# A third probability buffer and new ranks and spans in the order planner of a two-layer attention kernel

## What is computed

```python
# layer 0, per image: full attention over the 4096 positions, channels 64 for the scores
e1, e2, asm = prelu(w1 @ gn(x)), prelu(w2 @ gn(x)), prelu(wa @ gn(x))
x = x + softmax(e1.T @ e2) @ asm                      # 4096 x 4096 scores
# layer 1, per image: causal additive attention, 16 tanh units for each pair of positions
t = ln(tokens(x))
scores[i, j] = sum_a w2[a] * tanh(f[i, a] + g[j, a] + b1[a]) + b2      # only j < i is kept
t = t + (exp(scores) / sum) @ t
# gate (softmax over positions, top 8 for each of 64 experts), expert FFN, scatter back
```

## Time and profile before

| | us |
|---|---|
| median of three runs | 5871.09 (5862.58 to 5873.55) |
| the profiled execution | 5872.08 |
| its span, first to last instruction | 5869.9 |
| PE busy | 5078.5 (87%) |
| ACT busy | 4930.1 (84%) |
| DVE busy | 2663.9 (45%) |
| POOL busy | 2001.5 (34%) |

### The profile page before, as it was taken

The page is one execution under the profiler, slowest core; times in us unless marked ns, Lnnn a source line. Parts: engine busy times, 40 slices in busy tenths (PEclk is TensorE's granted clock), DMA queues, the critical chain, the costliest instruction groups (busy, mean ns, idle before and its releaser), DMA issues. The chain is left out here.

```text
span 5869.9 us, 71555 instructions
## 1 busy us (share of the span) xinstructions
PE 5078.5 (87%) x28567; PEld 1726.0 (29%) x28567; DVE 2663.9 (45%) x3558; ACT 4930.1 (84%) x4186; POOL 2001.5 (34%) x1643
## 2 busy tenths in 40 slices
PE   6999988889999978899999987889999987666657
PEld 2333332223333323222333333222333332111113
DVE  8853474433454466443453466443354454000132
ACT  0139969999989969999959969999978969999970
POOL 1474431125454431113464441112555451111110
PEclk8999999999999999999999999999999999888977
DMA  0000000000000010000000010000000010000028
GB/s 29 12 18 8 8 29 1 1 8 6 13 19 10 9 40 8 1 1 8 19 19 4 12 44 8 1 1 8 10 22 10 12 38 17 1 1 1 6 101 283
DMA packets 39418, 123.99 MB, mean 21 GB/s; under 512 B 4464, under 2 KB 5424, under 8 KB 31984
## 3 DMA queue, kind: packets, MB, share of 16 engines
q1 hardware_dynamic: 38272, 119.03, 6.1%
q10 hardware_dynamic: 816, 0.39, 0.0%
HBM read 89.85 MB, written 29.56 MB: 20 GB/s over the span
## 5 line engine op out<-in xcount | busy, mean ns | idle before, releaser
L890 ACT ACTIVATE tanh_slots<-query_part,key_part 128x2048 f32<-128x2048 f32 (+41 forms) x3072 | 4151.5, 1449 | 149.0 <-DVE key_part L1293 101.5
L946 PE MATMUL ps<-tanh_slots,packed 128*32 128x512 f32 (+2 forms) x18432 | 2080.7, 588 | 457.4 <-ACT tanh_slots L890 449.5
L846 POOL TENSOR_TENSOR context_and_exp_sums<-context_and_exp_sums,exp_scores 128x512 f32<-128x512 f32 (+3 forms) x544 | 632.8, 1185 | 2043.4 <-ACT exp_scores L902 1615.5
L946 PEld LDWEIGHTS ps<-tanh_slots,packed 128*32 128x32 f32 x18432 | 541.2, 113 | 1931.1 <-ACT tanh_slots L890 1094.3
L1369 DVE TENSOR_TENSOR _tokens_second_and_probs<-ps,e_and_minus_max 128x1024 f32<-128x1024 f32 x512 | 624.5, 1220 | 1059.5 <-PE ps L981 534.4
L859 POOL TENSOR_TENSOR conv_prob_sums<-conv_prob_sums,_tokens_second_and_probs 128x512 f32<-128x512 f32 x480 | 613.6, 1278 | 1151.6 <-ACT _tokens_second_and_probs L907 1146.5
L981 PE MATMUL ps<-_tokens_second_and_probs,asm_tokens 128*128 128x512 f32 x2048 | 995.6, 612 | 6.8 <-ACT _tokens_second_and_probs L907 6.8
L907 ACT ACTIVATE _tokens_second_and_probs<-_tokens_second_and_probs 128x1024 f32<-128x1024 f32 x512 | 549.2, 1073 | 454.2 <-DVE _tokens_second_and_probs L1369 454.1
L1345 DVE TENSOR_REDUCE row_max_parts<-ps 128x1 f32<-128x1024 f32 x512 | 608.4, 1220 | 452.6 <-PE ps L1060 440.6
L1205 DVE TENSOR_TENSOR context_and_exp_sums<-context_and_exp_sums,ps 128x512 f32<-128x512 f32 (+3 forms) x544 | 344.7, 638 | 717.6 <-PE ps L957 713.3
L861 POOL TENSOR_TENSOR conv_prob_sums<-conv_prob_sums,_tokens_second_and_probs 128x512 f32<-128x512 f32 x480 | 617.6, 1287 | 37.7
(11 more groups left out here) (156 smaller groups left out, 2062.4 us busy)
## 6 DMA issues: line engine op xcount, KB each, us to landing
y_scratch<-residual_chunks SPq DMA_DIRECT2D x64, 256.0 KB, 2.0
tanh_slots<-in_wg SPq DMA_DIRECT2D x16, 1024.0 KB, 10.5
residual_chunks<-y_scratch SPq DMA_DIRECT2D x63, 256.0 KB, 2.7
residual_chunks<-in_x SPq DMA_DIRECT2D x32, 256.0 KB, 2.8
e_and_minus_max<-p_scratch SPq DMA_DIRECT2D x32, 256.0 KB, 3.3
query_part<-in_x SPq DMA_DIRECT2D x4, 1024.0 KB, 6.0
normed_tokens_first<-in_x SPq DMA_DIRECT2D x4, 1024.0 KB, 8.5
p_scratch<-e_twice SPq DMA_DIRECT2D x4, 1024.0 KB, 6.8
```

The source lines that it names most:

```text
L846: pool.tensor_tensor(dst, dst, src, ALU.add).then_inc(s_ds, 1)
L890: nc.scalar.activation(S[:, 4 * (R % 2) + k, q:SUP], F[:, SUP * blk.s + q:SUP * blk.s + SUP], ACT.Tanh, bias=keypart(blk.b, kg, kg + 1)).t ...
L946: last = mm(PS[32 * k:32 * k + 32, t, off:CHUNK], w2k[:, g, :], S[:, 4 * (R % 2) + k, CHUNK * t + off:CHUNK * t + CHUNK], start=(g == 0), ...
```

## The change

A third probability buffer `XPB` is a tile of its own, and pair P uses buffer P mod 3; `SM` of pair P now waits for `PV` and `PS` of pair P-3. `QK` gets rank 2.5, so that on TensorE it goes ahead of `C`, `F2a`, the `L` steps and `M`, but not of TR. The spans given to the planner are new: tanh 0.19 us and not 0.1 beside the same slope, `E`, `K`, TR, `C`, `M`, `SM`, `EX` and `PS` by some hundredths, the HOP 0.12 and not 0.08. No instruction is added or removed.

```diff
+NPB = 3
-    HOP = 0.08
+    HOP = 0.12
-                prior_t = put("ACT", "T", (R, k), 0.1 + 0.833e-3 * (SUP - x.start(k, g)), behind, 4)
+                prior_t = put("ACT", "T", (R, k), 0.19 + 0.833e-3 * (SUP - x.start(k, g)), behind, 4)
-                prior_tr = put("PE", "TR", (R, t), 0.03 + 0.86 * w, behind, 2)
+                prior_tr = put("PE", "TR", (R, t), 0.02 + 0.89 * w, behind, 2)
-                put("PE", "QK", (P,), 1.1, behind, 4)
+                put("PE", "QK", (P,), 1.1, behind, 2.5)
-                if P >= 2:
-                    behind += [("PE", "PV", P - 2), ("POOL", "PS", P - 2)]
-                put("DVE", "SM", (P,), 1.25, behind, 1)
+                if P >= NPB:
+                    behind += [("PE", "PV", P - NPB), ("POOL", "PS", P - NPB)]
+                put("DVE", "SM", (P,), 1.2, behind, 1)
+        XPB = sb("probs_third", [128, 2, CHUNK])
+        PROBS = [PROB[:, 0, :, :], PROB[:, 1, :, :], XPB[:, :, :]]
-                z = PROB[:, P % 2, :, :]
+                z = PROBS[P % NPB]
-                if P >= 2:
-                    dve.wait_ge(s_pv, P - 1)
-                    dve.wait_ge(s_ps, P - 1)
+                if P >= NPB:
+                    dve.wait_ge(s_pv, P - NPB + 1)
+                    dve.wait_ge(s_ps, P - NPB + 1)
...
```

More of the change, by code:

```diff
@@ L252, in plan @@
             behind += [("PE", "C") + es[i - NEB], ("POOL", "D") + es[i - NEB]]
-        prior_e = put("ACT", "E", (n, t), 0.12 + 0.45 * w, behind, 1)
+        prior_e = put("ACT", "E", (n, t), 0.19 + 0.43 * w, behind, 1)
         done = [prior_e]
         if t == x.diag:
-            done.append(put("DVE", "K", (n, t), 0.35, [prior_e], 0))
-        put("PE", "C", (n, t), 0.05 + 0.86 * w, done, 3)
+            done.append(put("DVE", "K", (n, t), 0.3, [prior_e], 0))
+        put("PE", "C", (n, t), 0.07 + 0.88 * w, done, 3)
         behind = [("PE", "C", n, t)]
@@ L332, in conv @@
                     behind += [("PE", "M", b, 0), ("DVE", "M", b, NPAIR - 1 if b else 0)]
-                put("PE", "QK", (P,), 1.1, behind, 4)
+                put("PE", "QK", (P,), 1.1, behind, 2.5)
                 behind = [("PE", "QK", P), ("DVE", "SM", P - 1) if P else None, ("SP", "bc", b, c) if p == 0 else None]
-                if P >= 2:
-                    behind += [("PE", "PV", P - 2), ("POOL", "PS", P - 2)]
-                put("DVE", "SM", (P,), 1.25, behind, 1)
-                put("ACT", "EX", (P,), 1.0, [("DVE", "SM", P), ("ACT", "EX", P - 1) if P else None], 2)
+                if P >= NPB:
+                    behind += [("PE", "PV", P - NPB), ("POOL", "PS", P - NPB)]
+                put("DVE", "SM", (P,), 1.2, behind, 1)
+                put("ACT", "EX", (P,), 1.05, [("DVE", "SM", P), ("ACT", "EX", P - 1) if P else None], 2)
                 behind = [("ACT", "EX", P)]
@@ L343, in conv @@
                     behind.append(("PE", "F2a", (cc - 2) // NCH, (cc - 2) % NCH))
-                put("POOL", "PS", (P,), 2.6 if p else 1.3, behind, 3)
+                put("POOL", "PS", (P,), 2.7 if p else 1.3, behind, 3)
                 behind = [("ACT", "EX", P)]
@@ L404, in prep @@
             behind = [("DVE", "Ev", b, NCH - 1)] + max_free(b) if m == 0 else [("PE", "M", b, m - 1)]
-            put("PE", "M", (b, m), 0.9, behind + [("DVE", "M", b, m - 2) if m >= 2 else None], 4)
-            put("DVE", "M", (b, m), 1.25, [("PE", "M", b, m), ("DVE", "M", b, m - 1) if m else None], 4)
+            put("PE", "M", (b, m), 1.0, behind + [("DVE", "M", b, m - 2) if m >= 2 else None], 4)
+            put("DVE", "M", (b, m), 1.18, [("PE", "M", b, m), ("DVE", "M", b, m - 1) if m else None], 4)
         for i in range(parts(b)):
@@ L851, in PS_ @@
                 pool.wait_ge(s_pe, P + 1)
+                src = PROBS[P % NPB]
                 if p == 0:
@@ L980, in PV @@
                 for u in range(2):
-                    last = mm(PVB, VT[:, 2 * p + u, :], PROB[:, P % 2, u, :], start=(p == 0 and u == 0),
+                    last = mm(PVB, VT[:, 2 * p + u, :], PROBS[P % NPB][:, u, :], start=(p == 0 and u == 0),
                               stop=(p == PPC - 1 and u == 1))
```

8 lines of the change are left out of this document (4 added, 4 removed).

## The result

The changed kernel takes 5657.9 us (median of 4 runs, 5654.5 to 5662.1) against 5870.9 before: a ratio of 0.964, 95% interval 0.9623 to 0.9657. That is 213 us less; 124 were forecast, and the range ended at 5695. The direction held, the size did not.

The account below looks back on a forecast made before the run. TensorE's work ahead of each gate was the bound where ScalarE starves, ScalarE where TensorE idles. 24 x 2 + 16 + 64 - 4 = 124 us off 5872.1 gave 5748 us; range 5695 to 5835, leaving out a tenth each side.

Parts of the forecast that it names:

- What bounds the kernel: TensorE's work ahead of each gate where ScalarE starves, ScalarE where TensorE idles; moving pairs beside tanh gains.
- The cause, the tanh span,: Planner's full-tile tanh span, 1.81 us against 1.90 measured, put TR too early; TensorE stands 0.41 us before each group.
- The row-maximum stage: Beside second-half tanh: 12 `M` per key block for 11, hidden in idle; 32 us less, which pairs then fill.
- The gap and the stretch of pairs: Images 2 and 3: 13 more pairs ahead cut the 86.5 us gap to 47; 24 us gained each at 4% idle.
- The first one: Image 1's gap closes, with ten more pairs ahead of it: 16 us, bounds 5 and 21.
- The first halves: Four times: two pairs fewer 4 us, idle to 4% 7 us, chain 5 us; 16 us each, 64 together.
- The chain behind the last chunk: End of each first half: ten TR and two `C` inside gain 5 us; 22 us latency stays, nothing shortens it.
- The head: Before the first tanh: pays 4 us for two `QK` and one `PV` more before the first `L5`.
- The tail: The last 1,000 us, without pairs: 0 change, between -3 and +3 us.
- The mask: GpSimd mask operations: denser pairs make more masks wait, some 10 us of VectorE beside TensorE's path, left out of the sum.
- all goes as the counts say: Rival: idle near 1 or 2%, 5690 us, below 5700; chance 0.12.
- Exponentials: Rival: `EX` placed too early on ScalarE stalls tanh, then TR and `L5`; 5896 us at 0.4 us each; chance 0.06.

Follow-up runs that it names:

- the fastest kernel: Kernel before with tanh constant 0.215, third buffer and QK at rank 2.5, other spans and HOP of before: 5598.0 us (0.9537).

## Why the prediction was wrong

**What bounds the kernel** held. TensorE made up pairs in the gaps while it stood idle beside tanh, and the gain came from there: in the stretch of image 1's second half and image 2's first half its idle went from 98.3 + 31.8 us to 68.1 + 11.2. ScalarE's idle up to the last half image was to fall by about 120 us and fell by 206.

**The cause, the tanh span,** was named ("the old was 1.81", "TensorE stands before TR"), but only as the reason for the row-maximum stage and as a doubt about a rival. The sum took the counts of the whole order, and the text left the credit with "the third buffer and the later TR". Experiments gave the tanh constant by itself 213 us, as much as the whole change, and the buffer by itself 7, hardly clear of noise.

**The row-maximum stage** held: 12 `M` in a key block of 32.6 us, hidden. TensorE is idle 24.2 us of the 340.0, for 23 taken.

**The gap and the stretch of pairs** held in mechanism. The gap is 46.8 us (47 forecast). The idle that I took as 4% was 2.3%, 8.8 us for 15, which is most of why a second half and gap won 34.0 and 27.5 us and not 24. The first one won 16.6 for 16.

**The first halves are the step that failed**: "Idle of TensorE in the 367 us goes from 5.9% to the same 4%: 7 us", 16 us each with the rest, measured 37.3, 34.0, 30.1 and 30.4. I took one idle share for both kinds of half, carried over from the gap's row, and treated the tanh error as 5%. But the error is 0.09 us for each tile, whatever its length. A first half has 256 tiles of 1.18 us mean, an error of 23 us in some 300; a second half 512 tiles of 1.58, 46 in 810:

```profile
L890 ACT ACTIVATE tanh_slots<-query_part,key_part 128x2048 f32<-128x2048 f32 (+51 forms) x256 | 275.5, 1179 | 5.1 <-DVE key_part L1293 2.7 <-PE ps L946 2.4
```

(ScalarE's groups of the kernel before, 3089.5 to 3432.8 us.) The busy time of this row counts the end of a tile that the next instruction overlaps. Taken from the start of each tile to the start of what follows, waits left out, the 256 tiles are 267.8 us in the trace; the planner had 244.8 with 0.1 and has 267.9 with 0.19. For the 512 of a second half it is 753.1, 707.2 and 753.2. So 0.19 is right for short tiles and long ones. That this error costs first halves time of their own was shown by changing it there alone: 389.2 became 369.6 us, 20 for the 23 that the planner had wrong. Buffer and rank with the old spans took 7 us off the same half (382.3). The two together are near the 30 of the change, though no run shows that they add up. In image 1 pairs in hand may take part, as they do in the run with 0.19 in second halves alone. The whole idle of a first half, chain included, fell from 31.8 to 11.2 us, 3.1%; my own lower bound (none) had given 30 us. Its 9.5 us less work (357.4 to 347.9 busy) was more than the 4 of the two pairs' counts; an `FAa` and a `C` now stand behind `L5`, and the granted clock, 0.69 over the chain in the earlier trace rows, is 1.00 over the whole half now. How the 9.5 us divide among these was not measured.

**The chain behind the last chunk** was to stay late ("22 us of latency ... which nothing here shortens"). Tanh was laid beside all but 3 us of it. I counted ten TR as 5 us of TensorE's work, and should have counted them as ScalarE's tiles, which is what waited.

**The head** was -6.8 for -4, but not for the reason given. The kernel with buffer and rank and old spans has the same two `QK` and one `PV` more in that chain, and its first tanh starts at 434.0 us, against 432.2 before; with tanh 0.19, buffer and rank it is 432.8. It is 439.7 where the small spans and HOP are in as well without the tanh span, and 439.6 with the small spans but the old HOP; yet small spans, HOP and tanh span without buffer and rank give 433.8. So the small spans cost the head some 6 us, and only together with buffer and rank; HOP costs it nothing.

**The tail** won 8.0 us where I said 0, -3 to +3: from the start of the last half image to its last tanh it is 845 us and not 853. Not investigated.

**The mask**: 227/293/1373 ns least, median and longest, for 278/293/1368, and 75.1 us in all for 72.6. So the masks are 2.5 us longer in sum, and the median not at all. The Trainium skill's page SBUF — State Buffer (SBUF: two separate sides) has a VectorE operation with two SBUF inputs and a GpSimd operation that reads SBUF exclude each other. By that rule I had allowed some 10 us more of masks; the trace shows 2.5, and not what caused them.

**The rivals**: "all goes as the counts say" (5690, below 5700) had 0.12 and came nearest; with no idle at all the sum had been 5657. That this meets the measured 5657.9 is luck: idle is left everywhere, the first halves won more than that bound gave them (131.7 for 120), the later second halves less (61.6 for 78), and the tail 8 for 0. Exponentials did not stall tanh: ScalarE waited 21.0 us for scores from the first tanh of image 2 to its second half before, and 1.7 + 1.1 us now; the longest such waits lie in the head. The range reached down to 5695 although the bound of no idle, worked out at 5657, is what the text asked it to take in.

## What to carry to other kernels

Where an order is laid out by a planner, compare its span for the commonest stage with the trace first, as an error for each instruction and not as a share: 0.09 us on 3,072 tiles was 276 us of planner's error and 213 us of time. Then sweep that one number past the measured value too: it is also a knob for how far other work is packed ahead of that stage. Of the five values tried here the best was 0.215 for a measured 0.19; that it is best where neither of the two busiest engines runs dry first fits the traces but is not shown. Test the parts of a change one by one even when the whole gains: here two of them gained 25 us and two lost 26, unseen in the sum. A buffer more gains nothing clear of noise while the order doesn't use it. When a text has both ends of an unknown share, the range has to reach them.

## What the runs showed of the hardware

TensorE was kept busy through mixed work better than I took from the trace before: in the stretch of 509 us (2450 to 2959) of the fastest kernel, where TR, `C`, `QK` and `PV` alternate, it is busy 502.0 us, 98.6%. The granted clock fell where TensorE ran short of work. It is 1.00 from 2440 to 3006 us of the kernel with 0.24, buffer and rank. At the end of the first half behind it the pairs had run out: TensorE is busy 5.9 of 10 us from 3310 us on at a clock of 0.74, 6.1 of the next 10 at 0.50, and then all of 20 us, still at 0.50 (1.2 GHz), with ScalarE waiting for TR of a few short tiles there, up to 6.8 us at a time.

A tanh whose bias differs by partition occupies ScalarE, from start to start of the next instruction, for 0.19 us and 0.833 ns for each of its columns: that sum is 267.9 us for the 256 tiles of a first half and 753.2 us for the 512 of a second half, and the trace before has 267.8 and 753.1.
